# Expert rows added by DMA to a copy of x; the low parts of the experts' weights on VectorE

## The reference

```
xn  = layernorm(x)                                     # 2048 rows of 256
k, yh = xn @ W_z.T + b_z, xn @ W_h.T + b_h             # 256 x 256 each
log_h = cumsum over features of -softplus(k), plus a cumulative logsumexp over 1024 steps
log_h = (log_h - log_h.mean()) / std(log_h)            # over all tokens and features
attn  = layernorm(exp(log_h)[:, 1:] + xn) * ln_w + ln_b
p     = softmax(xn @ w_gate.T); the two largest of 8, divided by their sum
ffn   = sum over the two experts e of  p_e * ((silu(xn @ w1[e].T) * (xn @ w3[e].T)) @ w2[e].T)   # inner size 704
out   = x + attn + ffn
```

## Time and profile before

| | us |
|---|---|
| median of the timed runs | 379.75 |
| profiled execution, its own time | 378.11 |
| its span, first to last instruction | 376.2 |
| PE busy | 326.8 |
| VectorE busy | 265.1 |
| ScalarE busy | 216.4 |
| GpSimd busy | 198.8 |

### The profile page before, as it was taken

The page is one execution under the profiler, slowest core; times in us unless marked ns, Lnnn a source line. Parts: engine busy times, 40 slices in busy tenths (PEclk is TensorE's granted clock), DMA queues, the critical chain, the costliest instruction groups (busy, mean ns, idle before and its releaser), DMA issues.

```text
span 376.2 us, 6906 instructions
## 1 busy us (share of the span) xinstructions
PE 326.8 (87%) x1952; PEld 277.1 (74%) x1952; DVE 265.1 (70%) x479; ACT 216.4 (58%) x327; POOL 198.8 (53%) x212
## 2 busy tenths in 40 slices
PE   8997999839999999899999799999999698999400
PEld 8773555638887898798879698998999587888300
DVE  5378988898587759965899733465488957952166
ACT  2565998414889965897953279936723554233000
POOL 7500034086737777987788587637663856331200
PEclk9999989978999999999999899999999879999755
DMA  7795001043314321322143646412421001110379
GB/s 261 256 318 188 1 14 56 2 131 90 98 30 117 115 86 58 121 88 85 56 146 92 198 123 202 148 51 79 158 96 42 17 30 42 39 43 24 111 258 331
DMA packets 22012, 41.38 MB, mean 110 GB/s; under 512 B 2481, under 2 KB 15281, under 8 KB 21969
## 3 DMA queue, kind: packets, MB, share of 16 engines
q1 hardware_dynamic: 14784, 26.74, 22.5%
q0 software_dynamic: 3728, 10.10, 8.5%
q10 hardware_dynamic: 3456, 3.94, 3.2%
HBM read 31.60 MB, written 9.18 MB: 108 GB/s over the span
## 4 chain that ended last, share of the span: by engine, by line
PE 61%; DVE 20%; DMA 7%; ACT 6%; issue 4%; ACTq 1%; SPq 1%; DVEq 0%; POOL 0%; POOLq 0%
PE PS L1312 28%; PE PS L1327 16%; PE PS L1339 6%; PE PS L1206 5%; DMA small_sb<-small 2%; DVE xn L1059 2%; DMA y_dram<-hst,scol 2%; DMA raw<-w_tail 2%; DVE xn L1178 2%; ACT hT L588 2%; PE PS L1281 2%; DVE tmp L963 1%; DVE A L997 1%; DVE wbuf L778 1%; DVE hT L958 1%
## 5 line engine op out<-in xcount | busy, mean ns | idle before, releaser
L1312 PE MATMUL PS<-wbuf,xT 128*128 128x512 f32 (+1 forms) x648 | 151.3, 388 | 2.9 <-issue 2.3
L1312 PEld LDWEIGHTS PS<-wbuf,xT 128*128 128x128 f32 x648 | 119.9, 192 | 25.8 <-issue 5.2
L1327 PE MATMUL PS<-wbuf,hT 128*128 128x256 f32 x648 | 89.9, 294 | 2.5 <-DVE hT L958 2.4
L421 POOL TENSOR_TENSOR wbuf<-raw,wbuf x28 | 75.2, 2695 | 26.4 <-ACT wbuf L602 21.7
L1327 PEld LDWEIGHTS PS<-wbuf,hT 128*128 128x128 f32 x648 | 82.2, 195 | 4.8 <-issue 4.8
L958 DVE TENSOR_TENSOR hT<-PS,hT 128x768 fp32r<-128x768 f32 x36 | 34.4, 957 | 52.9 <-ACT hT L588 51.1
L402 POOL DMA_INDIRECT work<-xn_dram,gcol x39 | 42.7, 1095 | 29.9 <-POOL gcol L400 22.2
L593 ACT ACTIVATE tmp<-PS 128x512 f32<-128x512 f32 x72 | 32.0, 460 | 37.3 <-PE PS L1312 34.0
L410 POOL DMA_INDIRECT y_dram<-work,scol x35 | 38.5, 1100 | 27.5 <-POOL scol L408 25.2
L963 DVE TENSOR_TENSOR tmp<-tmp,PS 128x512 f32<-128x512 f32 x72 | 34.7, 514 | 24.0 <-ACT tmp L593 20.9
L1339 PE MATMUL PS<-ident,tmp 128*128 128x128 f32 x216 | 31.2, 283 | 13.9 <-DVE tmp L963 13.9
(11 more groups left out here) (196 smaller groups left out, 394.1 us busy)
## 6 DMA issues: line engine op xcount, KB each, us to landing
raw<-w_main SPq DMA_DIRECT2D x24, 544.0 KB
raw<-w_main SPq DMA_DIRECT2D x8, 416.0 KB
xn_dram<-xn SPq DMA_DIRECT2D x4, 512.0 KB, 8.6
U<-x ACTq DMA_DIRECT2D x2, 1024.0 KB
U<-y_dram SPq DMA_DIRECT2D x4, 512.0 KB, 7.0
A<-y_dram SPq DMA_DIRECT2D x4, 512.0 KB, 5.3
out<-xn SPq DMA_DIRECT2D x4, 512.0 KB, 3.5
xn<-x SPq DMA_DIRECT2D x4, 256.0 KB, 4.9
```

Of the source, the lines that this page charges most:

```text
L421: pool.tensor_tensor(lo, raw[:, ds(part, WP)], hi.bitcast(fp32), ALU.subtract).then_inc(s_w, 1)
L1312: ins = pe.matmul(PS[:, at:at + cols], xT[:, slot, xpart, q * P:(q + 1) * P], wbuf[:, w, wpart, q * 2 * F + at:q * 2 * F + at + cols], sta ...
L1327: ins = pe.matmul(y_ps, hT[:, hpart, c * P:(c + 1) * P], wbuf[:, w, wpart, W13 + c * D:W13 + (c + 1) * D], start=(c == 0 and hpart == 0 an ...
```

## The change

1. **Rows by DMA to the result.** `out` has 128 spare rows behind the tokens and is first filled with x by a DMA in DRAM (SP, after expert 0's weights). The weight of every slot is gathered with its row: `xrow` holds two columns more than `xn`, the token's two routing weights, and xn_dram's rows are 258 wide. DVE picks one of the two by `slot_weight`, ACT multiplies by it while it copies y, and `scatter` is an indirect DMA that adds to `out`. A scatter waits until the one before has landed (`rows_added`). `y_dram`, the loads of its halves, the 32 weighted additions and the four stores at the end are gone. The result of the last norm is added to `out` by four DMAs of 512 KB on POOL's queue (`add_attention`, before tiles 27, 29, 31 and after tile 32), each of which waits for the scatters before it and holds the ones behind it.
2. **Order at the front.** SP waits for its last load of x (`s_x[6]`) instead of the projections' weights before it loads expert 0. The routing weights are made right behind the picks, and the exponential for them stands in ACT behind `k_log(0)`; the four stores to xn_dram wait for them. DVE sorts a token's two experts no more. The initial state `u0` is finished ahead of tile 0's gate.
3. **POOL static.** All of POOL's tiles are written out; `gather` and `scatter` take their column from `gidx` and `sidx` directly, with no copy. POOL makes no low parts.
4. **Low parts by DVE.** `split_due` stands at the end of DVE's tile, with a register load and a branch in each.
5. **Attention branch.** `run_max` is cut in two, parts of it change between `between` and `after`, and most steps from tile 12 on come one tile earlier. `last_norm` has four scalar-tensor-tensors a pair of token tiles and adds no x. The two sums over all partitions stand behind `down` on PE.
6. **down** takes all products of h's high part first and waits for the low part behind them; twelve small matmuls (`warm`) stand ahead of the last `down`.

```diff
+        xrow = sb("xrow", [P, NT, XD])
+        xn = xrow[:, :, 0:D]
...
-            sp.wait_ge(s_large, 16)
+            sp.wait_ge(s_x[6], 16)
             for q in range(PIECES - 1):
                 sp.dma_start(raw[:, q * WP:(q + 1) * WP], w_main[0][:, q * WP:(q + 1) * WP]).then_inc(s_raw, 16)
             sp.dma_start(raw[:, WP * (PIECES - 1):WMAIN], w_main[0][:, WP * (PIECES - 1):WMAIN]).then_inc(s_raw, 16)
             sp.dma_start(raw[P - TAIL:P, WMAIN:WALL], w_tail[0]).then_inc(s_raw, 16)
+            sp.dma_start(out[0:NTOK, :].rearrange("(a r) d -> a (r d)", a=P),
+                         x.rearrange("(a r) d -> a (r d)", a=P)).then_inc(s_fill, 16)
+            sp.wait_ge(s_xn, NT - 4)
+            sp.wait_ge(s_xo, 4)
+            sp.wait_ge(s_rw, 1)
             for g in range(4):
-                sp.wait_ge(s_xn, 3 * g + 3)
-                sp.wait_ge(s_xo, g + 1)
                 sp.dma_start(xn_dram[512 * g:512 * (g + 1), :].rearrange("(t p) d -> p t d", p=P),
-                             xn[:, 4 * g:4 * g + 4, :]).then_inc(s_xnd, 16)
+                             xrow[:, 4 * g:4 * g + 4, :]).then_inc(s_xnd, 16)
...
-            sp.wait_ge(s_p2, 4 * NT // 2)
-            for k, buf in ((0, U), (1, A)):
-                sp.wait_ge(s_rows, k + 1)
-                for g in range(4):
-                    sp.dma_start(buf[:, 1024 * g:1024 * (g + 1)].rearrange("p (t d) -> p t d", d=D),
-                                 y_dram[k * NTOK + 512 * g:k * NTOK + 512 * (g + 1), :]
-                                 .rearrange("(t p) d -> p t d", p=P)).then_inc(s_yl[k][g], 16)
-            for g in range(4):
-                sp.wait_ge(s_fin, g + 1)
-                sp.dma_start(out[512 * g:512 * (g + 1), :].rearrange("(t p) d -> p t d", p=P),
-                             xn[:, 4 * g:4 * g + 4, :]).then_inc(s_out, 16)
-            sp.wait_ge(s_out, 64)
...
+            def gather(j):
+                if j >= DEEP:
+                    pool.wait_ge(s_xt, j - DEEP + 1)
+                    pool.wait_ge(s_ws, j - DEEP + 1)
+                k = j % DEEP
+                pool.indirect_dma_start(xg[:, k, :], None, xn_dram,
+                                        bass.IndirectOffsetOnAxis(gidx[:, j:j + 1], 0)).then_inc(s_gt[k], 16)
+            def rows_added(j, parts):
+                if j:
+                    pool.wait_ge(s_st, 16 * j)
+                if j == 0:
+                    pool.wait_ge(s_fill, 16)
+                if parts:
+                    pool.wait_ge(s_ab, 16 * parts)
+            def scatter(j, parts):
+                rows_added(j, parts)
+                pool.wait_ge(s_y, j + 2)
+                pool.indirect_dma_start(out, bass.IndirectOffsetOnAxis(sidx[:, j:j + 1], 0),
+                                        ysb[:, j % DEEP, :], None, compute_op=ALU.add).then_inc(s_st, 16)
+            def add_attention(j, m):
+                pool.wait_ge(s_p2, 4 * m + 4)
+                rows_added(j, m)
+                pool.dma_start(out[4 * m * P:4 * (m + 1) * P, :].rearrange("(t p) d -> p t d", p=P),
+                               xn[:, 4 * m:4 * m + 4, :], accum_op=ALU.add).then_inc(s_ab, 16)
+            for j in range(DEEP + 1):
+                gather(j)
             pool.wait_ge(s_idx, 1)
-            pool.wait_ge(s_xnd, 64)
-            def gather(j, k):
-                pool.tensor_copy(gcol[:, k:k + 1], gidx[:, ds(j, 1)]).then_inc(s_gc, 1)
-                hold(pool, s_gc, j + 1)
-                pool.indirect_dma_start(xg[:, k, :], None, xn_dram,
-                                        bass.IndirectOffsetOnAxis(gcol[:, k:k + 1], 0)).then_inc(s_gt[k], 16)
-            def scatter(j, k):
-                pool.wait_ge(s_y, j + 2)
-                pool.tensor_copy(scol[:, k:k + 1], sidx[:, ds(j, 1)]).then_inc(s_sc, 1)
-                hold(pool, s_sc, j + 1)
-                pool.indirect_dma_start(y_dram, bass.IndirectOffsetOnAxis(scol[:, k:k + 1], 0),
-                                        ysb[:, k, :], None).then_inc(s_st[k], 16)
...
+            def tile(i, u, parts=PARTS_OF_H):
                 j = LOOP * i + (1 + u)
-                if not isinstance(j, int) or j + DEEP < NTILES:
-                    pool.wait_ge(s_xt, j + 1)
-                    gather(j + DEEP, (1 + u) % DEEP)
-                scatter(j - 1, u)
-                if done is None:
-                    done = pool.value_load(plan[0:1, ds(j, 1)], min_val=0, max_val=PIECES * (E - 1))
-                return split_due(done, j)
-            def body(i):
-                done = pool.value_load(plan[0:1, ds(LOOP * i + 1, 1)], min_val=0, max_val=PIECES * (E - 1))
+                if j + DEEP < NTILES:
+                    gather(j + DEEP)
+                scatter(j - 1, parts)
...
+            added = 0
+            for i in range(8):
                 for u in range(LOOP):
-                    done = tile(i, u, done)
-            with pool.Fori(0, 8) as i:
-                body(i)
+                    j = LOOP * i + 1 + u
+                    if j in (27, 29, 31):
+                        add_attention(j - 1, added)
+                        added += 1
+                    tile(i, u, added)
+            add_attention(SURE - 1, added)
...
+                pool.tensor_copy(scol[:, 0:1], sidx[:, ds(used - 1, 1)]).then_inc(s_sc, 1)
+                pool.wait_ge(s_sc, 1)
+                pool.wait_ge(s_ab, 16 * PARTS_OF_H)
+                whole = pool.value_load(tiles_whole[0:1, 0:1], min_val=SURE - 1, max_val=NTILES - 1)
+                hold(pool, s_st, whole * 16)
+                hold(pool, s_y, used + 1)
+                pool.indirect_dma_start(out, bass.IndirectOffsetOnAxis(scol[:, 0:1], 0),
+                                        hst[:, 0:D], None, compute_op=ALU.add).then_inc(s_st, 16)
+                hold(pool, s_st, 16 * used)
...
+            def y_copy(j):
                 act.wait_ge(s_dn, j + 1)
-                act.wait_ge(s_st[u], value)
-                act.activation(ysb[:, u, :], y_ps, ACT.Copy).then_inc(s_y, 1)
+                act.wait_ge(s_ws, j + 1)
+                if j >= DEEP:
+                    act.wait_ge(s_st, 16 * (j - DEEP + 1))
+                act.activation(ysb[:, j % DEEP, :], y_ps, ACT.Copy, scale=wrow[:, j:j + 1]).then_inc(s_y, 1)
...
+                hold(act, s_ws, used)
+                act.activation(wrow[:, NCOL:NCOL + 1], wrow[:, ds(used - 1, 1)], ACT.Copy).then_inc(s_wl, 1)
+                act.wait_ge(s_wl, 1)
+                hold(act, s_dn, used)
+                act.activation(hst[:, 0:D], y_ps, ACT.Copy, scale=wrow[:, NCOL:NCOL + 1]).then_inc(s_y, 1)
...
+            dve.tensor_tensor(pick_b[:, :], hot1, hot2, ALU.add).then_inc(s_pick, 1)
+            dve.wait_ge(s_zex, 1)
+            step(dve.tensor_scalar(w12[:, 0, :], w12[:, 1, :], 1.0, None, ALU.add))
+            step(dve.reciprocal(xrow[:, :, D], w12[:, 0, :]))
+            dve.tensor_tensor(xrow[:, :, D + 1], w12[:, 1, :], xrow[:, :, D], ALU.mult).then_inc(s_rw, 1)
...
             def last_norm(m):
-                rows = xn[:, 2 * m:2 * m + 2, :]
                 for t in range(2 * m, 2 * m + 2):
-                    ins = dve.tensor_scalar(xn[:, t, :], xn[:, t, :], mv[:, t, 0:1], rstd[:, t:t + 1],
-                                            ALU.subtract, ALU.mult)
+                    ins = dve.scalar_tensor_tensor(xn[:, t, :], xn[:, t, :], mv[:, t, 0:1], lnwb[:, 0, :],
+                                                   ALU.subtract, ALU.mult)
                 ins.then_inc(s_p2, 1)
-                dve.wait_ge(s_p2, 4 * m + 1)
-                for k in range(2):
-                    dve.tensor_tensor(rows, rows, lnwb[:, k:k + 1, :].to_broadcast([P, 2, D]),
-                                      ALU.add if k else ALU.mult).then_inc(s_p2, 1)
-                    dve.wait_ge(s_p2, 4 * m + (2 + k))
-                dve.wait_ge(s_xre, 32)
-                dve.tensor_tensor(rows, rows, xre[:, 2 * m:2 * m + 2, :], ALU.add).then_inc(s_p2, 1)
+                dve.wait_ge(s_p2, 2 * m + 1)
+                for t in range(2 * m, 2 * m + 2):
+                    ins = dve.scalar_tensor_tensor(xn[:, t, :], xn[:, t, :], rstd[:, t:t + 1], lnwb[:, 1, :],
+                                                   ALU.mult, ALU.add)
+                ins.then_inc(s_p2, 1)
+            def slot_weight(j):
+                k = j % DEEP
+                dve.wait_ge(s_gt[k], 16 * (j // DEEP + 1))
+                dve.scalar_tensor_tensor(wrow[:, j:j + 1], xg[:, k, D:D + 1], first_pick[:, j:j + 1],
...
+            def split_due(before, j):
+                done = dve.value_load(plan[0:1, ds(j + 1, 1)], min_val=0, max_val=PIECES * (E - 1))
+                with dve.If(before < done):
+                    with dve.Fori(before, done) as p:
+                        part = dve.snap(p % PIECES * WP)
+                        hold(dve, s_hi, p + (PIECES + 1))
+                        lo, hi = (wslot(p // PIECES + 1, n, part) for n in (1, 0))
```

(97 more changed lines are left out.)

188 lines of the change are left out of this document (66 added, 122 removed).

## The result

The changed kernel took **359.76 us** (median of four runs, 357.17 to 361.19) against 379.72 us for the kernel before on the same chip. The ratio is 0.947, with a 95% interval of 0.940 to 0.953. The profiled execution took 359.08 us with a span of 357.1; before, the span was 376.2. The forecast was 347.0 with a range of 338 to 363. So the direction and the range held, and the change brought 19.1 us of span where the steps had promised 32.2.

The account below looks back on a forecast made before the run. PE was taken as the bound in most of the tile loop, with idle time at DVE's gate, front and end. 378.1 - 1.4 - 2.9 - 7.0 - 20.9 = 345.9 us, as a median 347; range 338 to 363.

Parts of the forecast that it names:

- DVE becomes the bound: Rival in the loop: no gain there and 5 us lost, 357.9 us, as a median 359.5; chance 0.22.
- End: After tile 35's transposes: the 28.9 us become 8.0, a gain of 20.9 us.
- +0.95 us: At the end, the last `down` needs h's high part alone and starts +0.95 after the transposes, before 2.4 us.
- From `down`'s end to the scatter's issue: At the end, without POOL's column copy this stretch takes 0.85 us instead of 1.5.
- The landing: At the end, the last adding scatter lands in 4.0 us; 7.17 or 2.45 would make the gain 16.0 or 22.5.
- the links: Each adding scatter waits for the one before; all but the last counted as hidden, while a link is below 6.9 us.
- Loop: Tile loop: 15.5 us of stalls and slow work go, 8.5 us of late gates come, net gain 7.0 us.
- my signs: What would show it; for the gate, PE waits at tiles 10 to 20 and 28 of about 1 us, none near 4.
- The low parts hide: Rival in the loop: ACT reaches its high part earlier, all 15.5 us kept, 337.4 us, median 339; chance 0.15.
- the chain of scatters: Rival: 40 dependent links bind from 79.3 us on; 7.4 us a link equals the old time, 9.4 gives 459; chance 0.07.
- Front: Before tile 0: earlier weights and logits cut PE's 2.6 us wait for the picks; gain 1.4 us, the middle.
- Tiles 0 to 2: Behind tile 0, DVE's chain takes 3.0 us instead of 6.3, u0 costs 0.4; gain 2.9 us, PE's gap about 3.

Follow-up runs that it names:

- experiment 8: Changed kernel without the twelve idle matmuls ahead of the last `down`: 358.11 us, ratio 0.945.
- experiment 6: Changed kernel, low parts behind the next tile's gate, last normalisation's pieces 4, 5 in tile 29 and 6, 7 in tile 30, attention parts added earlier: 353.39 us.
- experiment 7: Changed kernel, low parts behind the next tile's gate, scatters plain (overwriting) instead of adding, so the result leaves out the sum: 349.79 us, ratio 0.924.
- experiment 12: Changed kernel, low parts behind next gate, normalisation pieces 4, 5 in tile 29 and 6, 7 in 30, parts added earlier, SyncE awaiting last landing: 353.94 us.
- experiment 5: The changed kernel itself measured again, nothing altered: 358.23 us, ratio 0.946.
- experiment 10: Changed kernel with the front edit undone, so SyncE again waits for the large constants before expert 0's weights: 358.68 us, ratio 0.945.
- experiment 1: Changed kernel with DVE's low parts behind the next tile's gate, x's low part and slot weight instead of ahead of that gate: 354.56 us, ratio 0.933.
- experiment 11: Kernel before the change with only the low parts moved, to DVE behind the next tile's gate: 366.47 us, ratio 0.962.
- experiment 3: Changed kernel with SyncE instead of GpSimd waiting for the last adding scatter's landing: 358.49 us, ratio 0.944.
- experiment 2: Changed kernel with the low parts made by GpSimd again, behind the tile's scatter: 356.48 us, ratio 0.939.

## Why the prediction was right or wrong

**Right in direction, and in range by luck.** Of the 13.1 us between the forecast gain and the measured one, 7.4 lie at the end, 6.7 in the loop and 1.25 at the front; tiles 0 to 2 gave 2.2 back. The measured time lies in the range because its upper end stood for "DVE becomes the bound", which is not what happened.

**End, the largest miss.** Three terms failed and one held.
- `down` was to start +0.95 us behind the transposes "with the high part alone"; it started +3.1. I took the 2.4 us before it for h's low part, because the chain of waits had that row there. But that row only ran beside the cause, by experiment 8: with `down` no longer behind the low part, and with or without the idle matmuls, PE stands still for 1.6 to 2.6 us all the same. At full clock `down` took 2.38 us and not 2.14, which was the chain's piece of an earlier one. Together 2.4 us.
- From `down`'s end to the scatter's issue: 1.68 instead of 0.85 us. In experiments 6, 7 and 12, where the last scatter waited for the copy alone, it was 1.33 to 1.35, so 0.5 us is a term that I had too small and 0.35 is the scatter ahead, which landed last. I counted the links as hidden; that holds for the loop and fails where the loop ends, behind added parts that each hold the next scatter back for 6.9 us.
- The landing, taken as 4.0, measured 3.83. Of its bounds 7.17 was read from a row; for 2.45 I named none, and the plain scatter of experiment 7 then gave 2.41.
- The drain of 4.1 to 4.4 us was in no step. The kernel before has one of 6.52 us in its trace, hidden beside SyncE's and VectorE's last work. When I took that work away I had to ask what it covered.

**Loop: 15.5 us of gain, 8.5 of cost, net 7.0; measured 13.0, 12.7 and 0.3.** The gain's mechanism held (tiles 18 and 29 to 31). Of the cost, 8.0 us have the mechanism that was named, a low part ahead of the gate waiting for ACT, but I priced it at one mean tile, tile 20, times nine. Tiles 5, 14 and 19 paid 1.5, 2.7 and 1.4 us. Behind tile 14's gap of 2.1 us the next `up` took 5.57 us, and 5.56 in experiment 5; behind the same gap it took 4.10 in experiments 8 and 10, so the slow stretch does not follow from the gap alone. The 4.7 us in tiles 12, 17, 20 and 21 that stay in experiment 1 have another source: in experiment 11, with the old order of the attention branch and no slot weights, these tiles take 6.88, 7.17, 6.86 and 7.42 us instead of 7.65, 8.65, 8.25 and 8.15. I had counted the new order as free. Of my signs, PE's waits near 1 us were seen at tiles 5, 10, 19 and 29; tile 14's of 2.1 us was over what I had allowed.

**"DVE becomes the bound" gave 359.5 us, nearest to the result, and is refuted as a mechanism.** Its price was a loop 5 us longer; it was 0.3 us shorter, and DVE is busy for 189 of its 254 us. Experiments 1 and 11 give the same work another place and take 8.0 and 19.5 us off the loop. Where it is true is in three tiles of experiment 1 (13, 15 and 17). The number agreed because the end was 7.4 us worse.

**"The low parts hide" (339) could be had in the loop for about half by moving two lines:** experiment 1's loop is 8.3 us shorter than the loop before, against the 15.5 us of that rival. The end then took 3.8 us of it, since the chain of scatters became the bound behind part 3. So the chain did bind, but only over the last part (6.9 us) and the last links (4.0 to 5.1 us), not over all 40; the links are far from the 7.4 us each that would have eaten the gain.

**Front.** The step's value of 1.4 us was wrong (0.15), its cause too: undoing SyncE's wait costs nothing (experiment 10). The picks come 2.6 us earlier, 2.3 of them without that edit, and then PE loses 1.0 us to ACT and about 1.0 us to the clock. The eleven traces of the changed kernel and its versions, whose front code is nearly one, show the clock's share: where the mean granted clock from 44 to 56 us is 0.86 (experiments 5, 6, 7, 8 and 10), tile 0 starts at 61.93 to 62.51 us; where it is 0.72 (the changed kernel and the other five), at 62.99 to 63.71. No edit sets it, since experiment 5 is the changed kernel itself. At 0.86, which the kernel before had too, this step would have measured about 1.2 us.

**Tiles 0 to 2.** 5.1 us instead of 2.9. The predicted mechanism is there: DVE's chain behind tile 0 is shorter, and tile 1 takes 9.63 us instead of 13.59, 4.0 us of gain. PE's gap of 5.92 us is 0.47, but that is too good a picture, since tile 1's `up` was slow and filled the wait. The changed kernel first, then experiment 8:

```profile
70.37 5.66 PE L1297 MATMUL PS<-wbuf,xT 128*128 128x512 f32 x18 [1.19 <-issue]
...
78.84 0.87 PE L1327 MATMUL PS<-ident,tmp 128*128 128x128 f32 x6 [0.47 <-DVE tmp L945]
```
```profile
69.30 4.11 PE L1297 MATMUL PS<-wbuf,xT 128*128 128x512 f32 x18 [1.21 <-issue]
...
77.75 0.87 PE L1327 MATMUL PS<-ident,tmp 128*128 128x128 f32 x6 [2.00 <-DVE tmp L945]
```

At the full clock the gap is 2.0 us, where I had said about 3, and the tile is as long (9.60 to 9.66 us in the five traces with this order of the low parts). The other 1.1 us is tile 2, 7.62 us instead of 8.75, because the slow stretch fell into tile 1, where it costs nothing. That is luck: in experiments 3, 8 and 10 it fell into tile 2, which then took 8.4 us.

**What the whole is made of.** Moving the low parts alone, in the good place, is worth 14.6 us in the kernel before; experiment 1 against before is 25.6 us. So about 11 us belong to the rows added by DMA and the rest of the change, most of it at the end and none in the loop (experiment 11). As made, the change had 20.0: the place of the low parts cost it 5.2.

## What to carry to other kernels

When work moves to an engine with slack, its place in that engine's order decides before its length does: put it behind the instruction that the bounding engine waits for next, not ahead of it, above all if it waits for a third engine. When the last work of a kernel goes, list what ran beside it (drains, branch exits, chains of dependent transfers), because these are the new end. A price for a moved wait has to be worked out tile by tile; the mean hides the ones that cost.

## What the runs showed of the hardware

- An indirect scatter of 128 rows of 1 KB that adds takes 1.56 us to issue at the end of the kernel (1.71 in the mean of 35) and is seen landed 3.8 us after the issue began; a plain one takes 0.98 and 2.41 us (experiment 7). At best, dependent ones follow each other at 4.0 to 4.1 us and, plain, at 2.9 us. Behind an added part of 512 KB the next scatter was issued 6.9 to 7.0 us later in the changed kernel.
- GpSimd's drain at the end lasts 4.12 us behind an adding scatter that was waited for (seven kernels), 6.52 to 6.53 in the four with plain scatters, and 7.27 to 7.36 when its record starts just before the last issue (three). In the versions of the changed kernel its end lies 7.05 to 9.0 us behind the last issue. What it does is open. The records (start us, us, operation), the changed kernel, the plain scatters and experiment 3:

```
348.88 1.572 DMA_INDIRECT   352.71 wait met   352.76 4.117 DRAIN
338.02 0.983 DMA_INDIRECT   340.43 wait met   340.48 6.526 DRAIN
349.62 1.572 DMA_INDIRECT                     349.4  7.265 DRAIN
```

- Where TensorE leaves the nested branches, 1.6 to 2.6 us pass between the last transpose's end and the next matmul (1.6 in experiment 2, 2.2 in 5, 2.4 in the changed kernel, 2.6 in 8). That the branches are the cause is by exclusion (experiment 8).
- The same TensorE instructions are granted the full clock in one execution and not in another. Up to its last `down` the code of experiment 8 is the changed kernel's; tile 1's `up` took 4.11 us there and 5.66 here, tile 15's 4.10 and 5.57. The last `down` took 2.38 us in the changed kernel and 3.62 and 3.27 in experiments 6 and 12, whose PE code is the same but whose loop is timed otherwise. So about 1.5 us at such a place in one trace can belong to no edit.
